# Output-projection matmuls issued one loop step earlier in an 8-core attention and feed-forward layer

## The reference

```python
# x: (4, 4096, 1024) float32; heads 16, key and value width 64, one key/value head for all
x = x + attn(layernorm(x))
x = x + ffn(layernorm(x))

# attn: r = input
q = einsum('bnd,hkd->bnhk', r, query_proj); k = r @ key_proj; v = r @ value_proj
attn = softmax(einsum('bnhk,bmk->bnhm', q, k) / sqrt(64))
o = einsum('bnhm,bmv->bnhv', attn, v)
out = einsum('bnhv,dhv->bnd', o, output_proj)

# ffn: a scalar function for each of 64 units
s = x @ Win + bin_
h = relu(s[..., None] * W1 + b1)          # 16 inner values a unit
g = einsum('btmh,mh->btm', h, W2) + b2
out = g @ Wout + bout
```

## Time and profile before

| what | us |
|---|---|
| median of 3 runs (1604.83 to 1606.13) | 1605.78 |
| the profiled execution | 1607.38 |
| span of its slowest core (core 1) | 1605.8 |
| spans of the 8 cores | 1595.6 to 1605.8 |
| ScalarE busy | 1192.0 (74%) |
| TensorE busy (matmuls) | 1146.8 (71%) |
| VectorE busy | 315.1 (20%) |

### The profile page before, as it was taken

The page is one execution under the profiler, slowest core; times in us unless marked ns, Lnnn a source line. Parts: engine busy times, 40 slices in busy tenths (PEclk is TensorE's granted clock), DMA queues, the critical chain, the costliest instruction groups (busy, mean ns, idle before and its releaser), DMA issues.

```text
span 1605.8 us, 22038 instructions; the slowest of 8 cores (1595.6 to 1605.8 us)
## 1 busy us (share of the span) xinstructions
PE 1146.8 (71%) x7488; PEld 419.9 (26%) x7488; DVE 315.1 (20%) x456; ACT 1192.0 (74%) x1491; POOL 94.6 (6%) x188
## 2 busy tenths in 40 slices
PE   0786577777777777777777777777777725575565
PEld 0443322222222222222222222222222201232211
DVE  2454411000012000011100110110110013423332
ACT  3556689999999999999999999999999922523310
POOL 0000000000001000000100010010010002000000
PEclk9998599999999999999999999999999967877655
DMA  7313230000002000000300000020000024353343
GB/s 212 120 56 134 71 105 1 1 1 1 1 1 83 9 10 9 9 3 3 82 9 9 10 10 4 22 62 9 10 17 3 3 66 130 133 166 110 118 144 92
DMA packets 33949, 81.83 MB, mean 51 GB/s; under 512 B 10224, under 2 KB 11248, under 8 KB 32880
## 3 DMA queue, kind: packets, MB, share of 16 engines
q1 hardware_dynamic: 25136, 60.88, 12.6%
q0 software_dynamic: 8704, 19.54, 3.8%
HBM read 60.34 MB, written 25.17 MB: 53 GB/s over the span
## 4 chain that ended last, share of the span: by engine, by line
PE 39%; ACT 35%; issue 10%; DMA 7%; DVE 6%; SPq 1%; ACTq 1%; DVEq 0%; POOL 0%; POOLq 0%
ACT ptu L514 31%; PE spb L499 10%; PE oAe L538 7%; PE oBe L538 6%; PE qps L350 3%; PE spa L499 2%; PE fo L687 2%; DMA x2d<-big 2%; PE op_ps L764 2%; PE oBo L538 2%; DMA ot<-r1u 2%; DVE big L556 1%; DMA big<-wq 1%; ACT hfp L659 1%; PE kps L323 1%
## 5 line engine op out<-in xcount | busy, mean ns | idle before, releaser
L514 ACT ACTIVATE ptu<-spb 128x1024 bf16<-128x1024 f32 x512 | 524.5, 1024 | 71.3 <-PE oBo L538 27.2
L514 ACT ACTIVATE ptu<-spa 128x1024 bf16<-128x1024 f32 x512 | 522.9, 1021 | 21.2 <-PE oBo L538 10.3
L538 PE MATMUL oBo<-ptu,vab 64*65 64x512 bf16 x1024 | 386.4, 377 | 2.7
L538 PE MATMUL oAe<-ptu,vab 64*65 64x512 bf16 x1024 | 382.1, 373 | 6.4 <-DVE big L556 6.2
L538 PE MATMUL oAo<-ptu,vab 64*65 64x512 bf16 x1024 | 385.9, 377 | 0.0
L538 PE MATMUL oBe<-ptu,vab 64*65 64x512 bf16 x1024 | 383.7, 375 | 0.3 <-DVE big L556 0.2
L499 PE MATMUL spb<-qt,k2t 64*128 64x512 bf16 x1024 | 201.9, 381 | 158.2 <-ACT ptu L514 154.2
L499 PE MATMUL spa<-qt,k2t 64*128 64x512 bf16 x1024 | 201.6, 381 | 66.0 <-ACT ptu L514 25.7
L553 DVE COPY big<-oBo 65x512 f32<-65x512 f32 x32 | 22.0, 687 | 846.8 <-PE oBo L538 846.8
L499 PEld LDWEIGHTS spb<-qt,k2t 64*128 64x128 bf16 x1024 | 64.1, 92 | 380.1 <-issue 380.1
L499 PEld LDWEIGHTS spa<-qt,k2t 64*128 64x128 bf16 x1024 | 64.0, 92 | 289.9 <-issue 289.9
(11 more groups left out here) (64 smaller groups left out, 764.4 us busy)
## 6 DMA issues: line engine op xcount, KB each, us to landing
xbuf<-x_own SPq DMA_DIRECT2D x32, 512.0 KB, 4.7
xbuf<-x_oth SPq DMA_DIRECT2D x16, 512.0 KB, 4.5
rcpb<-zscr POOLq DMA_DIRECT2D x64, 128.0 KB, 2.7
x2d<-big POOLq DMA_DIRECT2D x16, 512.0 KB, 4.4
big<-x2d SPq DMA_DIRECT2D x32, 256.0 KB, 4.4
out<-big SPq DMA_DIRECT2D x32, 256.0 KB, 2.6
zscr<-zscr SPq DMA_DIRECT2D x60, 128.0 KB, 3.2
big<-wq SPq DMA_DIRECT2D x8, 512.0 KB, 9.0
```

The lines of the kernel that those rows point to most:

```text
L514: expT[gmc] = S.emit("scalar", lambda s_, gmc=gmc: s_.activation(ptu[:, gmc % 7, :], sp[gmc % 2][:], AF.Exp, scale=0.125), waits=ew, inc=" ...
L538: tgt = S.emit("tensor", lambda te, ob=ob, rg=rg, col=col, mc=mc, gmc=gmc: te.matmul(ob[:], vab[rg:rg + 64, mc, :], ptu[rg:rg + 64, gmc % ...
```

## The change

The projection matmuls of tile t+1 are issued in step t in place of those of tile t; in step 0 those of tiles 0 and 1 both. The waits of a tile's matmuls are the same expressions, and so are all other instructions.

```diff
@@ -748,8 +748,9 @@
                     xw += bwC["sync"]
                 xload_t[('C', t)] = S.emit("sync", lambda e, t=t, q=q: e.dma_start(
                     xbuf[:, q, :], x_tiles[0][t]), waits=xw, inc=wsem4[q], inc_n=16)
-            t = step
-            if t < 16:
+            for t in ([0] if step == 0 else []) + [step + 1]:
+                if t >= 16:
+                    continue
                 q = t % 4
                 sm = wsem4[q]
                 mw = [("dve", x2add_t.get(t - 2, 0)),
```

## The result

The changed kernel took 1659.65 us (median of 10 runs, 1656.04 to 1661.64) against 1606.47 us of the kernel before (10 runs on the same chips). The ratio is 1.0323, with a 95% interval from 1.0305 to 1.0342: on the 1606 us of the kernel before that is 52 us slower, where +51.9 and 1657 us were forecast. The profiled execution took 1657.1 us, the span of its slowest core (core 2) is 1655.6 us, 49.8 more than before.

The account below looks back on a forecast made before the run. Attention fills three quarters of the span; in stage C/D residual adds wait for the spill, final adds for fo. Terms 51.8 - 3.6 + 3.0 + 0.7 = +51.9 us on 1605.78 give 1657 us, range 1646 to 1670 (8 in 10: 1641 to 1675).

Parts of the forecast that it names:

- The ring: Stage C/D from step 8: spill lands, residual add, projection, fo, final add, copy, normalise, spill; seven steps +51.8 us.
- x2add(7): VectorE's residual add of tile 7, in stage C/D; from step 8 on these adds wait for the spill.
- The gap of 9.83 us in steps 8 to 14: Residual add to final add in stage C/D: 1.35 to projection start, 5.60 projection, 2.88 to final add.
- mm: A tile's 16 projection matmuls on TensorE, taken as 5.60 us in steps 8 to 14.
- the full-clock 3.62: Time in us of a tile's 16 projection matmuls at full clock; would make the sum 13.9 us less.
- the rival in which the clock stays low through them: Clock stays low through projection and fo matmuls, steps 8 to 14: +25 us, 1682 us; chance 0.06.
- Flight of the spill: Spill issue to residual add start, 4.15 us in step 8 and 6.81 in step 9; kept unchanged.
- The rival in which transfers spread in the longer steps: Transfers spread, up to 2.7 us won in each of five steps, or clock holds better: 1643 to 1644 us; chance 0.06.
- Step 15, -3.6 us: Last projection moves to step 14, so final add follows residual add in 1.14 us in place of 4.78.
- s2ps(0), +3.0 us: Step 7: the first s2ps matmuls start later, behind tile 8's projection, delaying the feed-forward chain 3.0 us.
- Step 4, +0.7, and steps 5 to 7, nothing: Step 4: transposes end later behind tile 4's projection, +0.7 us; steps 5 to 7: both fit in 6.74 us.
- Faster and no-change rivals: Faster: fo passes the waiting projection, -12.7 us, 1593 us, chance 0.02; no change: projection fits into slack, 1606 us, 0.02.

Follow-up runs that it names:

- second and third experiments: Second: changed kernel with early projection matmuls moved behind fo and s2ps, 1590.96 us; third: kernel before with fo and s2ps ahead of projection, nothing early, 1598.99 us, ratio 0.9914.
- the kernel with both obstacles away: Changed kernel with early projection matmuls moved behind fo and s2ps, and five residual slots in place of three: 1576.93 us, ratio 0.9771 to the kernel before.
- its partner with nothing early: Kernel before with fo and s2ps ahead of the projection, which stays in its own step, and five residual slots: 1574.98 us, ratio 0.9755.

## Why the prediction was right

The ring from x2add(7) to x2add(15) took 118.42 us before (1408.51 to 1526.93 and the same view) and 168.26 us after (1407.91 to 1576.17): 49.8 us, the whole difference of the two spans. The other parts of stage C/D nearly cancel: x2add(2) to x2add(7) 45.2 us in both, x2add(15) to the last final add 70.0 before, 70.5 after. These are the slowest cores of one profile each, core 1 before and core 2 after. On cores 0, 2, 4 and 6, each against itself, the ring grew by 45.4 to 51.2 us. The mechanism is the same on all of them, but the deviations of 1 to 3 us per term below are no larger than this spread.

- **The gap of 9.83 us in steps 8 to 14.** Measured 9.28 to 10.75, mean 10.28, so seven steps gave 71.96 us where the sum had 68.8. The mis-sized term is mainly mm: 5.9 us in the mean, not 5.60, +2.1 us in seven steps (in step 10 one record is missing, and the start is put where the other steps have it). The way from the end of mm to the final add was 2.9 to 3.1 us where 2.88 was said, +0.8, and x2add to the start of mm 1.37 to 1.48 where 1.35 was said, +0.2. The windows view of step 10 has a granted clock of 0.59 against the 0.72 of the earlier trace rows, but over 20 us with more standing in them:

```profile
1441.00:1461.00 20.00, 9.50 (x29) 3.65 (x30) 2.93 (x4) 3.50 (x9) 0.53 (x1) 0.59 0.34 105
```

  A finer cut of step 9 shows the clock of the burst itself: 0.50 through the stand and the first 4 us of the burst (1422.4 to 1434.0 us), 0.66 to its end at 1436.4, and 1.00 in the fo matmuls behind it. The two rows that the 5.60 was taken from were too few: the seven bursts take 4.9 to 6.5 us. The length of the stand does not order them: the longest burst (6.5 us, step 8) follows the shortest stand (3.9 us). The rule on bursts after a DMA wait (the Trainium skill, "TensorE: Matmul & The Clock Gate", HAM oscillation) pointed the right way: the full-clock 3.62 did not occur from step 8 on. The fo matmuls stayed fast (1.12 us for two) in steps 8 to 14, so the rival in which the clock stays low through them did not come.
- **Flight of the spill.** Kept as it was; in steps 9 to 16 it sums to 46.1 us after and 47.9 before: -1.8 us. It is two steps that make it up: 7.07 us against 8.16 in step 10, 3.04 against 3.94 in step 16. The rival in which transfers spread in the longer steps, up to 2.7 us in each of five, did not come: 6.86 us against 6.81 in step 9, 7.15 against 7.38 in step 11, 7.34 against 7.33 in step 13. The transfers on SP are released together either way: output, x tile and reload start 1.3 to 2.7 us after the final add of step 8 does, before and after.
- **Step 15, -3.6 us.** From 4.78 to 1.44: -3.3.
- **s2ps(0), +3.0 us.** From x2add(6) to s2ps it was 1.96 us, and is 4.82 (1388.43 to 1393.25), +2.9:

```profile
1389.80 3.61 PE L765 MATMUL op_ps<-wq_wp,ot 128*128 128x512 bf16 x16 [2.31 <-DVE big L737]
1393.25 1.89 PE L653 MATMUL s2ps<-qt,win2b 128*128 128x512 bf16 x8
```

- **Step 4, +0.7, and steps 5 to 7, nothing.** Missed by a little: the residual adds from step 4 to step 7 lie 18.9 us apart, not 20.7. The +0.7 of step 4 did not come: the transposes ended at 1369.75 and took 0.61 us where 1.0 was said, and the copy (1370.68) followed the residual add (1369.54) at once. The spill flew 3.1 to 3.2 us in place of 3.6 to 4.1 in steps 5 to 7. Why is not settled; that projection and spill start at other times from each other in this order is only an argument. With the shorter flight of step 8 (3.06 us against 4.15) this cancelled the 2.9 us of s2ps.
- **Faster and no-change rivals.** `fo` stood behind the held projection in all seven steps. What the faster rival would have had from TensorE, the second and third experiments got by writing the order down: forecast 1593 us, measured 1591 (and by the ratio 1592).

The misses are +3.2 us in the gaps of steps 8 to 14, +0.3 in step 15, -0.1 in s2ps, -1.8 in the flights of steps 9 to 16, -1.1 in that of step 8 and -2.5 in steps 4 to 7. They sum to -2.0; the spans give -2.1 (49.8 against 51.9). The mechanism held; that the sum came closer than its terms is luck.

## What to carry to other kernels

Issuing work earlier on an engine that runs in order also moves its wait earlier, and all that stands behind it inherits that wait. Ask first whether anyone waits for the work (here nobody did), and then what stands behind it. In a software pipeline the instruction with the latest input belongs last in the step: behind `fo`, the same early matmuls were free. A resource that costs little in the old order, here the three slots (about 9 us, all of it ahead of step 8), sets how much such a misplaced wait costs: 52 us with three slots, nothing that shows with five.

## What the runs showed of the hardware that was not expected

A burst of 16 matmuls of 128x512 took 4.9 to 6.5 us in each of steps 8 to 14 of the changed kernel, where TensorE had stood 3.9 to 8.3 us ahead of it, and in step 9 the granted clock was back at 1.00 only for the fo matmuls behind it. In the kernel with both obstacles away, bursts at the full clock come back in two of these steps, among others that take 4.2 to 5.9 us:

```profile
1404.72 3.63 PE L778 MATMUL op_ps<-wq_wp,ot 128*128 128x512 bf16 x16
...
1412.66 5.31 PE L778 MATMUL op_ps<-wq_wp,ot 128*128 128x512 bf16 x16
```

In its partner with nothing early, five of the bursts of steps 8 to 15 take 3.6 us, one 3.9 and two 6.3 to 6.4. A tighter ring thus gives back some of the clock as well, up to 2.3 us a step (5.9 less 3.63), but not in every step; how much of the last two kernels' gain is clock was not separated.
